# A Perceiver block: the second residual sum transposed through DRAM and VectorE, and the first tiles in another order

## The reference

```python
x = x + attention(layernorm(x), ctx, ctx, mask)
u = layernorm(x)
x = x + irfft(rfft(u, 2048) * rfft(K, 2048))[..., :1024] + D * u   # K: the S4 kernel of length 1024
z = layernorm(x)
scores = (z @ Wq.T) @ keys.T                        # 64 per row
gate = softmax of the 16 largest scores, else 0
x = x + ((z @ A.T) * gate, each over 8 columns) @ B.T * 2
```

## Time and profile before

| | us |
|---|---|
| median of 3 runs | 1307.82 |
| lowest and highest | 1303.91, 1310.32 |
| profiled execution | 1306.38 |
| its span, first to last instruction | 1304.6 |
| TensorE busy (share of the span) | 1243.8 (95%) |
| ScalarE | 1117.4 (86%) |
| VectorE | 1057.6 (81%) |
| GpSimd | 827.7 (63%) |
| DMA engines, mean busy share over the span | 47% |

### The profile page before, as it was taken

One profiled execution on the slowest core, in us unless ns is written; L12 is line 12 of the kernel. 1 busy time (PEld: TensorE's weight loads), 2 busy tenths in 40 slices (PEclk: granted clock), 3 DMA queues, 4 the chain that ended last, 5 costly groups with the idle time before them and its releaser, 6 DMA issues.

```text
span 1304.6 us, 42153 instructions
## 1 busy us (share of the span) xinstructions
PE 1243.8 (95%) x13676; PEld 1078.2 (83%) x13676; DVE 1057.6 (81%) x3560; ACT 1117.4 (86%) x3329; POOL 827.7 (63%) x1259
## 2 busy tenths in 40 slices
PE   2579999999999999999999999999999999999997
PEld 2457888888888888888888888888888888888876
DVE  6988888888888887888888888887888888888753
ACT  3689989989999998999999898988999898998841
POOL 5437667666666776666677666667766666776420
PEclk9979999999999999999999999999999999999999
DMA  8544454454455455445545454454545445554210
GB/s 211 138 121 121 136 150 121 128 145 130 124 133 140 121 136 137 134 125 131 137 120 146 127 148 117 125 137 128 141 125 145 125 121 141 127 142 120 61 59 33
DMA packets 270940, 166.45 MB, mean 128 GB/s; under 512 B 195433, under 2 KB 253298, under 8 KB 270722
## 3 DMA queue, kind: packets, MB, share of 16 engines
q1 hardware_dynamic: 270722, 163.74, 46.7%
HBM read 128.50 MB, written 34.08 MB: 125 GB/s over the span
## 4 chain that ended last, share of the span: by engine, by line
PE 85%; DVE 4%; SPq 3%; ACT 2%; issue 2%; DMA 2%; POOL 1%; DVEq 0%; POOLq 0%; ACTq 0%
PE ps_p L565 25%; PE ps_p L651 15%; PE ps_p L636 15%; PE ps_p L664 14%; PE ps_p L597 9%; PE ps_s L577 8%; SPq L384 2%; ACT pr L832 1%; DVE ms L1395 1%; DMA dn<-den 1%; DMA turn<-lasts 1%; DVE x L1250 0%; POOL lastp L1095 0%; ACT pts L784 0%; SPq L431 0%
## 5 line engine op out<-in xcount | busy, mean ns | idle before, releaser
L832 ACT ACTIVATE pr<-ms,negmax 128x256 f32<-128x256 f32 x1024 | 513.9, 504 | 12.0 <-DVE negmax L1395 11.9
L1395 DVE CUSTOM_DVE_ANT_0 ms<-ps_s,neg_mask,last 128x256 f32<-128x256 f32 x1024 | 456.6, 470 | 35.4 <-PE ps_s L577 29.9
L784 ACT ACTIVATE pts<-ps_p 128x512 f32<-128x512 f32 x512 | 295.9, 592 | 48.3 <-PE ps_p L565 44.2
L565 PE MATMUL ps_p<-ident,pr 128*128 128x128 f32 x2048 | 306.2, 278 | 9.4 <-DVE wa_lo L1195 4.5
L565 PEld LDWEIGHTS ps_p<-ident,pr 128*128 128x128 f32 x2048 | 240.1, 141 | 44.7 <-issue 16.7
L832 ACT ACTIVATION_READ_ACCUMULATOR pr<-ms,negmax 128x1 f32 x1024 | 199.8, 195 | 0.0
L1053 POOL TENSOR_TENSOR kt<-kr,kt 128x512 fp32r<-128x512 f32 x128 | 165.1, 1290 | 28.4 <-ACT kt L784 27.9
L651 PE MATMUL ps_p<-wa_hi,ut_hi 128*128 128x288 f32 x512 | 177.6, 347 | 1.6 <-DVE ut_lo L1195 1.6
L651 PE MATMUL ps_p<-wa_lo,ut_hi 128*128 128x288 f32 x512 | 151.2, 295 | 0.0
L651 PE MATMUL ps_p<-wa_hi,ut_lo 128*128 128x288 f32 x512 | 150.6, 294 | 0.0
L1095 POOL TENSOR_TENSOR lastp<-lastp 128x256 f32<-128x256 f32 (+4 forms) x320 | 129.7, 405 | 22.7
(11 more groups left out here) (140 smaller groups left out, 2717.3 us busy)
## 6 DMA issues: line engine op xcount, KB each, us to landing
kx<-in_ctx SPq DMA_DIRECT2D x512, 64.0 KB, 2.4
cx<-in_ctx SPq DMA_DIRECT2D x128, 256.0 KB, 3.1
xq<-in_x SPq DMA_DIRECT2D x32, 512.0 KB, 4.3
turn_q<-xq SPq DMA_DIRECT2D x32, 512.0 KB, 3.8
qx<-turn_q SPq DMA_DIRECT2D x128, 128.0 KB, 2.9
xr<-in_x SPq DMA_DIRECT2D x32, 512.0 KB, 4.3
out_x<-tmp SPq DMA_DIRECT2D x32, 512.0 KB, 5.2
dn<-den SPq DMA_DIRECT2D x512, 2.0 KB, 2.2
```

The costliest lines, as they stand in the source:

```text
L565: mm = pe.transpose(into[:, j * P:(j + 1) * P], source, ident[:, :])
L784: return act.activation(out, in_, ACT.Copy, scale=scale)
L832: act.activation(pr[:, b % 2, g, :], ms[:, n % MS, :], ACT.Exp, bias=negmax[:, n % MS:n % MS + 1], scale=-1.0, accum_out=den[:, b, g:g + 1 ...
L1395: dve.tensor_tensor_reduce(ms[:, n % MS, :], ps_s[:, g % GPH, g // GPH * SW:(g // GPH + 1) * SW], neg_mask[:, 0:SW], 1.0, last[:, it % 2, ...
```

## The change

- `z_chunk` is gone. `store_z` writes `x2s` to a new DRAM tensor `turn_z`; `move_z` reads it back into the new buffer `zq`, 1 KB pieces, as `move_q` does. `z_turn` on VectorE transposes 32x32 blocks, half a tile a call, reading with a step of 8 floats, into `zr`, which shares the memory of `zg`. The features then stand in another order, so the weights A and the router weights are transposed from columns with the same step of 8.
- `z_high` reads `zr` in SBUF. `z_low` is GpSimd's. `z_turn` of the second half waits for `z_low` of the first.
- `un` is dropped; `row_norm` writes into `xr`, and `load_residual` waits for `u_chunk`.
- In the set-up the mask, the centring of the weights (`query_centre`, `weight_centre`) and two products with `wide` are ScalarE's instead of VectorE's.
- All orders and the table `BANKS` are new. In the loop TensorE starts `experts` of tile `it - 2` after `scores(it, 1)`, and `expand(it - 2, 1)` and the second half of `third_residual` fall into the next pass. At the start ten `weight_chunk` (of 16) stand before `scores(0, 0)`; before there were three. At the end `u_chunk(31)` and `convolve(31)` stand before `expand(30)`, and `experts(30, 1)` mostly after `attend(31, 7)`.

VectorE's, around the first maxima: `maximum` 0 to 3, `z_turn(it - 2, 0)`, `q_stats`, `third_residual(it - 3, 1)`, `maximum` 4 and 5, `z_turn(it - 2, 1)`, `maximum` 6, `normalisers`, `maximum` 7, 8, 9. SP's: `store_last`, `load_x`, `load_keys`, `store_z`, `turn_last`, `move_z`, two `move_den`, `store`. The core of the diff:

```diff
-        un = sb("un", [P, DIM])
+        zq = sb("zq", [P, DIM])
...
+        zx = zq[:].rearrange("p (b d c) -> p c b d", b=BPT, c=FC)
+        zr = zg[:].rearrange("p (c t) -> p c t", c=FC // 2)
...
+            def store_z(tile, odd):
+                sp.wait_ge(x2_done, at(tile, 2, 2))
+                if at(tile, 64, 0) > 0:
+                    sp.wait_ge(z_moved, at(tile, 64, 0))
+                sp.dma_start(turn_z.rearrange("b s c -> (b s) c"), x2s[:, odd, :]).then_inc(z_stored, 16)
+
+            def move_z(tile):
+                sp.wait_ge(z_stored, at(tile, 16, 16))
+                if at(tile, 2, 0) > 0:
+                    sp.wait_ge(zr_done, at(tile, 2, 0))
+                for quad in range(GPH):
+                    sp.dma_start(zq[SEQ * quad:SEQ * (quad + 1), :].rearrange("p (b f) -> p b f", b=BPT),
+                                 turn_z.rearrange("b s (q f) -> s b q f", q=GPH)[:, :, quad, :]).then_inc(z_moved, 16)
...
             def load_residual(tile):
-                if at(tile, 4, 0) > 0:
-                    sp.wait_ge(tm_done, at(tile, 4, 0))
+                if at(tile, 2, 0) > 0:
+                    sp.wait_ge(ut_done, at(tile, 2, 0))
...
+                    store_z(it - 3, 1 - odd)
+                if on(it - 1):
+                    turn_last(it - 1)
+                if on(it - 3):
+                    move_z(it - 3)
+                if on(it - 2):
...
             def u_chunk(tile, h):
                 pe.wait_ge(u_ready, at(tile, 1, 1))
-                transposes([un[:, (4 * h + j) * P:(4 * h + j + 1) * P] for j in range(4)],
+                transposes([xr[:, (4 * h + j) * P:(4 * h + j + 1) * P] for j in range(4)],
                            "u", h, tile, ut_done, ul_done, at(tile, 2, h + 1))
-
-            def z_chunk(tile, h, odd):
-                pe.wait_ge(x2_done, at(tile, 2, h + 1))
-                transposes([x2s[:, odd, (4 * h + j) * P:(4 * h + j + 1) * P] for j in range(4)],
-                           "z", h, tile, zt_done, zl_done, at(tile, 2, h + 1))
...
+            keys_transpose(); weight_chunk(0, 0); router_product(); weight_chunk(0, 1); weight_chunk(1, 0)
+            cauchy_sums(); weight_chunk(1, 1); weight_chunk(2, 0); weight_chunk(2, 1); weight_chunk(3, 0)
+            weight_chunk(3, 1); weight_chunk(4, 0); weight_chunk(4, 1); scores(0, 0); dft_product()
...
+            def weight_centre(j):
+                act.wait_ge(a_mean, j + 1)
+                act.activation(stages[STAGE[j]], stages[STAGE[j]], ACT.Identity, scale=-float(DIM),
+                               bias=row_mean[:, j:j + 1]).then_inc(a_centred, 1)
...
+            def wide_products():
+                act.wait_ge(wide_loaded, 32)
+                act.wait_ge(su_s4, 2)
+                for j in range(2):
+                    act.activation(work[j], wide[2], ACT.Copy, scale=lam[:, j:j + 1]).then_inc(su_wide, 1)
...
             def row_norm(tile):
                 act.wait_ge(rstd_step[1], at(tile, 3, 3))
-                if at(tile, 2, 0) > 0:
-                    act.wait_ge(ut_done, at(tile, 2, 0))
-                act.activation(un[:, :], x1[:, :], ACT.Identity, bias=lns[1][:, 14:15],
+                act.wait_ge(tm_done, at(tile, 4, 4))
+                act.activation(xr[:, :], x1[:, :], ACT.Identity, bias=lns[1][:, 14:15],
                                scale=lns[1][:, 15:16]).then_inc(u_ready, 1)
...
             def z_high(tile, h):
-                act.wait_ge(zt_done, at(tile, 2, h + 1))
+                act.wait_ge(zr_done, at(tile, 2, h + 1))
                 act.wait_ge(y_done, at(tile, 2, 2))
-                copy(ut_hi[:, 4 * h:4 * h + 4, :], product("z", h, tile)[:].rearrange("p (c t) -> p c t", c=4)).then_inc(zh_done, 1)
+                copy(ut_hi[:, 4 * h:4 * h + 4, :], zr[:, :, :]).then_inc(zh_done, 1)
...
+            def z_low(tile, h):
+                pool.wait_ge(zh_done, at(tile, 2, h + 1))
+                pool.tensor_tensor(ut_lo[:, 4 * h:4 * h + 4, :], zr[:, :, :], ut_hi[:, 4 * h:4 * h + 4, :].bitcast(F32),
+                                   ALU.subtract).then_inc(zl_done, 1)
...
-            def z_low(tile, h):
-                dve.wait_ge(zh_done, at(tile, 2, h + 1))
-                split(ut_lo[:, 4 * h:4 * h + 4, :], product("z", h, tile)[:].rearrange("p (c t) -> p c t", c=4),
-                      ut_hi[:, 4 * h:4 * h + 4, :], zl_done)
+            def z_turn(tile, h):
+                dve.wait_ge(z_moved, at(tile, 64, 64))
+                dve.wait_ge(zl_done, at(tile, 2, h))
+                if at(tile, 1, 0) > 0:
+                    dve.wait_ge(gt_done, at(tile, 1, 0))
+                dve.transpose(zr.rearrange("p c (b s) -> p c b s", b=BPT),
+                              zx[:, 4 * h:4 * h + 4, :, :]).then_inc(zr_done, 1)
...
             def second_residual(tile, h, odd):
                 dve.wait_ge(y_done, at(tile, 2, h + 1))
+                if at(tile, 16, -16) > 0:
+                    dve.wait_ge(z_stored, at(tile, 16, -16))
```

734 lines of the change are left out of this document (367 added, 367 removed).

## The result

The changed kernel takes 1373.6 us, the median of four executions (1373.4 to 1378.3), beside 1306.6 us of the kernel before on the same chip. The ratio is 1.052, with an interval of 1.048 to 1.056: slower by 67 us, where the prediction said some 21 us faster. The profiled execution, the slowest of the four, took 1378.3 us; its span is 1376.5 us, 71.9 us over the span before.

A forecast was written before the change was run, and what follows sets the result against it. TensorE was taken to bound the loop, busy throughout each 37.7 us pass, and mostly VectorE the first tiles. On the span 1304.6 - 31.9 + 6 + 8.4 - 2.1 + 2 - 4 = 1283.0 us; predicted time 1286 us, range 1270 to 1308.

The forecast's parts named there:

- Part 2: Loop: work moved to VectorE, ScalarE, GpSimd and SP stays below the 36.7 us pass; waits cost 6 us in all.
- The rival of other waits: Loop: waits other than the late bounce eat the gain, 0.5 us a pass more, 1301 us (1296 to 1312); chance 0.12.
- The price of the strided read: z_turn on VectorE and the weights' transposes: reading at a step of eight floats adds nothing, z_turn staying at 0.70 us.
- The rival that held it: Loop: strided read makes VectorE the bound, deciding from 4.0 us for each z_turn, about 1367 us; chance 0.04.
- The bounce as a deadline: Loop: z's trip through DRAM takes 14.6 us from convolution to low half, under 15.5 us of TensorE work, 0.9 to spare.
- its rival: Loop: the bounce lands late, 0.8 us a pass more, 1309 us (1300 to 1330); chance 0.13.
- Part 1: Loop: transposes leaving TensorE save 1.03 us a tile, 31.9 us over 31 tiles; pass becomes 36.70 us.
- Part 3: Last tile: net +8.4 us from two gaps, -2.1 us for experts products moved later, +2 us for a slow clock.
- the slow clock: Last tile: TensorE idling lowers the granted clock for the matmuls after it, +2 us, bounds 0 to 5.
- The two gaps: Last tile: attention to convolution 3.4 us shorter, convolution to experts 11.8 us longer, net +8.4 us.
- Part 4: First tiles: VectorE sheds 8.7 us, scores(0, 0) comes up to 6.5 us later; -4 us, bounds -8.7 and +6.5.
- The rule set aside: Whole change: skill rule sends 128x128 transposes to TensorE where PSUM is fine, leaving 1307.8 us; judged not borne out here.

The follow-up runs named there:

- e8: e5 with the normalisers behind maximum 7 instead of ahead of it: 1331.9 us, ratio 1.020.
- e5: Changed kernel with the second residual's sum written by quad, block, feature and weights in natural order, so z_turn reads densely, computation whole: 1363.2 us, ratio 1.043.
- e3: Changed kernel with z_turn reading 512 neighbouring floats instead of every eighth, features in a wrong order: 1353.5 us, ratio 1.038.
- e1: Changed kernel with the normalisers ahead of the second half's z_turn instead of behind it: 1404.9 us, ratio 1.076.
- e2: Changed kernel with the second half's z_turn behind maximum 7, experts waiting for that half only before the fifth of eight blocks: 1367.8 us, ratio 1.049.
- e17: e16 with the first z_turn behind one statistic of x and ScalarE's copy behind exp 3: 1326.0 us, ratio 1.017.
- e6: Changed kernel without the bounce's five transfers, turns reading the second residual's own tile, features in a wrong place: 1354.6 us, ratio 1.037.
- e11: e9 with SyncE's order changed: third denominator ahead of the bounce's reads, fourth keys ahead of the fourth denominator: 1394.4 us, ratio 1.070.
- e16: e9 with the third denominator's four transfers split: one ahead of the bounce's store, one ahead of its reads, two behind: 1321.1 us, ratio 1.014.
- e14: e9 without the bounce's five transfers, turns reading the second residual's own tile densely, features in a wrong place: 1306.6 us, ratio 1.002.
- e9: e8 with the last tile's second sum turned by TensorE, as before the change: 1328.6 us, ratio 1.018.
- e12: e9 with both turns later, behind the third residual and two statistics, ScalarE's copies and GpSimd's low halves following: 1402.0 us, ratio 1.076.

## Why the prediction was wrong

- **Part 2, "so it costs nothing while TensorE covers it", is the step that failed.** It put TensorE's waits in the loop at 6 us; they were 76.5 us, 41.7 of them at the border. The sums of a pass were near (VectorE 33.1 us for 31.1, GpSimd 28.25 for 28.3, ScalarE 34.8 for 34.3), and all were below the pass. But they were sums. VectorE has no slack between `scores(it, 0)` and maximum 7, where the change had put both turns, `third_residual` and the normalisers. I saw that the normalisers no longer stood behind maximum 7 and took the border to be bare; they had moved ahead of it, where it was overfull. Putting them back behind it took the scores' wait from 34.0 to 2.2 us (e8 against e5). The rival of other waits had it at 0.5 us a pass (chance 0.12). The forecast of the loop was -31.9 + 6 = -25.9 us, and it gave +54.4.
- **The price of the strided read was taken as nothing**; it is 0.44 us a turn, 0.8 to 0.9 us a pass with both turns ahead of the border (e3). The rival that held it let it decide from 4.0 us a turn, when VectorE's whole pass is full. It cost time at 1.15 us already. The rule cited from the Trainium skill (SBUF — State Buffer, the box on cachelines in its section on Door 1) has its direction borne out by e3 and e5, on VectorE; TensorE's weights were not measured.
- **A product whose neighbour I changed became six times as dear**, 193 ns alone and 1160 beside `z_low`. Moving the normalisers, with this product, out from ahead of the border is worth 0.84 us a pass (e8 against e5). The term was in no sum. The earlier trace rows gave GpSimd's new work a price on GpSimd and none on its neighbour. The Trainium skill has the rule (SBUF — State Buffer, Who interferes with whom: a VectorE instruction with two SBUF inputs contends with a GpSimd one that reads SBUF, and whoever comes second is blocked); e1 and e2 agree with it (193 ns), and so does the kernel after, where the product ends 0.04 us behind the subtraction that had started 0.15 us ahead of it.
- **The bounce as a deadline** was right in the mean, and its rival right in kind: the experts do not wait in the loop. But there was no room: `z_low` of the second half ends at 602.87, and the experts start at 604.37 only because the border had held TensorE for 1.44 us. Without that wait they would start at about 602.93, by these rows. With the second turn a little later they waited once more in each pass, for a copy of ScalarE's behind it (e1, e17). Where the bounce was late it stopped VectorE, 19 times, and through `third_residual` the attend, 0.53 us a pass (e6), and by filling SyncE's queue the transfers behind it (e1, e11, e16).
- **Part 1**: 1.03 us of transposes was 0.71 us of TensorE's time (e14). Start-to-start distances in the chain were the source. What fills the other 0.3 us isn't settled. Another 0.49 us a pass went into two small waits of the new order, which no sum had.
- **Part 3**: +16.5 us for 8.3. The wait from convolution to experts was right (14.1 for 14.6), the slow clock wasn't: experts and `expand` took 9.07 + 7.34 us against 6.63 + 5.74 before, 4.0 us for the 2. The two gaps gave 7.1 us for 8.4. The other 5.4 us lie between `scores(31, 0)` and the end of the last attention (45.1 to 50.5 us), where 2.1 us less was forecast. TensorE waits for 5.3 us there, and for 0.3 before; 2.2 of it is the experts' wait for `ut_lo` of tile 30, whose turn waits 3.73 us for its transfer. So the bounce of tile 30 was late as well, and the sum had only the last tile's.
- **Part 4**: +1.0 us for -4, inside the bounds. VectorE's work from 33 to 66 us did fall, from 32.18 to 28.22 us, but the first tiles did not get shorter; the granted clock there was 0.69 for 0.89, and no run separates the two.
- **The rule set aside**: the prediction said that the trace did not bear out leaving the transposes to TensorE, since TensorE had no idle time. No version here beats the kernel that leaves them there.

So the sign turned on the loop. With strided read, place and last tile mended (e9) the kernel is still 1.8% slower than before, and even without the bounce's transfers (e14) it is no faster, 1.0022 (1.0007 to 1.0038). The best version that computes everything is e16, 1321.1 us, 1.4% slower than the kernel before. What keeps most of its passes between 37.5 and 39.4 us was shown only in part: the queue (e16) and the moment of the turn, from both sides (e12, e17). The DMA engines' own load was not tried, and the keys land late even without the bounce (e14). Nor were the set-up changes and the dropping of `un` tried alone.

## What to carry to other kernels

Sum each engine's work between two borders of a single buffer, not over a pass: work that fitted the pass with 6 us to spare stopped TensorE for 1.44 us in each. When work goes to another engine, ask whom it meets there in time, and what the new transfers are queued ahead of. Before a reorder that gives a late input more time, look at what the instruction in front was covering.

## What the runs showed of the hardware

- VectorE's 32x32 transposes of 128x512 floats read at a step of 8 floats take 1151 ns, dense ones 699 to 711 ns (after, e3, e5).
- A VectorE product of two SBUF inputs of 32 columns took 1160 ns when it was issued 0.15 us behind GpSimd's 1275 ns subtraction of two SBUF inputs, ended 0.04 us behind it, and took 193 ns away from it (after, 28 of 32 tiles; e1, e2).
- In a steady loop with a single long TensorE wait of 2.08 us a pass, the granted clock fell to 0.53 for 3.4 us, in 24 of 29 passes (e12).
